# 64-token attention: the length product of a rotation one step later, its logarithm and exponential behind the next pair's exponentials

## The reference, cut to what matters

```python
h = shift_token(x)
q, k, v = split(h @ wqkv)               # 8 heads of 64
q = q / clip(norm(q, axis=-1), 1e-12) * qs   # the length of each head's row
k = k / clip(norm(k, axis=-1), 1e-12) * ksc
q, k = rotary_xpos(q, k)
sim = (q * 8) @ k'                      # own and previous window of 64 tokens
attn = softmax(where(mask, -big, sim))
x = x + (attn @ v) @ wo
...                                     # shift, layer norm, gated MLP
```

## Time and profile before

| | |
|---|---|
| median of 3 runs | 2924.2 us (2923.81 to 2928.21) |
| profiled execution, its time | 2927.47 us |
| its span in the trace | 2924.8 us |
| PE busy | 2709.7 us, 93% |
| DVE, ACT, POOL busy | 1950.3, 1877.3, 1051.4 us |
| rotations, lengths, pairs | 128 of each, in four layers |

### The profile page before, as it was taken

The page is one execution under the profiler, slowest core; times in us unless marked ns, Lnnn a source line. Parts: engine busy times, 40 slices in busy tenths (PEclk is TensorE's granted clock), DMA queues, the critical chain, the costliest instruction groups (busy, mean ns, idle before and its releaser), DMA issues.

```text
span 2924.8 us, 63475 instructions
## 1 busy us (share of the span) xinstructions
PE 2709.7 (93%) x24100; PEld 1851.9 (63%) x24100; DVE 1950.3 (67%) x5625; ACT 1877.3 (64%) x4404; POOL 1051.4 (36%) x876
## 2 busy tenths in 40 slices
PE   8989999978999999789999999898899998998998
PEld 5655656547888887368888887355455463554554
DVE  5554646366887885678888887675576325774774
ACT  5676767504766764157777776776687514875784
POOL 2322323202333330055555552454355013552551
PEclk8999999987999998899999999999999999999999
DMA  1010000000000000200000000310111002110210
GB/s 54 1 42 1 13 1 9 4 9 1 2 2 2 2 2 3 75 1 2 2 2 2 2 2 15 118 48 19 48 49 28 23 1 59 48 34 23 53 42 15
DMA packets 35280, 63.13 MB, mean 22 GB/s; under 512 B 11526, under 2 KB 15654, under 8 KB 33830
## 3 DMA queue, kind: packets, MB, share of 16 engines
q1 hardware_dynamic: 34982, 59.07, 7.3%
HBM read 23.48 MB, written 1.15 MB: 8 GB/s over the span
## 4 chain that ended last, share of the span: by engine, by line
PE 71%; DVE 13%; ACT 8%; issue 4%; SPq 2%; POOL 2%; DMA 1%; DVEq 0%; POOLq 0%; ACTq 0%
PE bank L787 61%; PE bank L1018 5%; PE bank L1138 3%; SPq L753 2%; PE bank L863 1%; ACT low L1344 1%; DVE low L1686 1%; ACT work L1380 1%; DVE low L1664 1%; DVE work L1629 1%; ACT work L1288 1%; DMA work<-work 1%; DVE halves L1679 1%; ACT squared L1260 1%; DVE centered L1500 1%
## 5 line engine op out<-in xcount | busy, mean ns | idle before, releaser
L1256 ACT ACTIVATE low<-bank 128x512 f32<-128x512 f32 (+3 forms) x512 | 427.9, 946 | 1.7 <-PE bank L1018 1.7
L787 PE MATMUL bank<-table_keys,halves 128*128 128x512 f32 (+3 forms) x1536 | 422.6, 384 | 0.6 <-ACT low L1344 0.5
L787 PE MATMUL bank<-work 128*64 128x128 f32 (+6 forms) x4480 | 365.3, 291 | 39.8 <-DVE work L1773 20.1
L1344 ACT ACTIVATE low<-bank,low 128x512 f32<-128x512 f32 (+23 forms) x384 | 227.2, 592 | 270.5 <-DVE low L1686 266.7
L787 PEld LDWEIGHTS bank<-work 128*64 128x64 f32 (+3 forms) x4480 | 266.1, 145 | 211.9 <-issue 152.2
L1686 DVE TENSOR_REDUCE low<-bank 128x1 f32<-128x512 f32 (+22 forms) x512 | 286.4, 570 | 104.0 <-PE bank L787 99.0
L1877 POOL TENSOR_TENSOR halves<-squared,const 128x512 fp32r<-128x512 f32 x128 | 136.9, 1069 | 518.9 <-PE bank L787 518.9
L1256 ACT ACTIVATE work<-bank 128x512 f32<-128x512 f32 (+4 forms) x389 | 199.7, 538 | 156.4 <-PE bank L787 80.0
L787 PEld LDWEIGHTS bank<-table_keys,halves 128*128 128x128 f32 x1536 | 248.6, 194 | 47.5 <-issue 14.0
L1380 ACT ACTIVATE work<-work 128x192 f32<-128x192 f32 (+1 forms) x512 | 218.7, 431 | 38.6 <-DVE work L1766 38.6
L1923 POOL TENSOR_TENSOR work<-work 128x768 f32<-128x768 f32 x128 | 187.7, 1466 | 135.7 <-DVE work L1777 135.7
(11 more groups left out here) (200 smaller groups left out, 5805.5 us busy)
## 6 DMA issues: line engine op xcount, KB each, us to landing
work<-work SPq DMA_DIRECT2D x512, 64.0 KB, 2.0
slot<-in_wW SPq DMA_DIRECT2D x4, 1605.5 KB, 6.6
slot<-in_wA SPq DMA_DIRECT2D x4, 837.0 KB, 6.1
table_low<-embv_padded SPq DMA_DIRECT2D x2, 1536.0 KB, 6.3
table<-in_dft SPq DMA_DIRECT2D x1, 3072.0 KB, 13.3
slot<-in_wE SPq DMA_DIRECT2D x2, 584.0 KB, 3.8
const<-in_const SPq DMA_DIRECT2D x1, 1094.5 KB, 5.5
squared<-in_x SPq DMA_DIRECT2D x4, 256.0 KB, 6.5
```

Source lines behind the costliest of these rows:

```text
L787: return pe.matmul(o, l, r, start=start, stop=stop)
L1256: return act.activation(dst, src, ACT.Identity)
L1344: act.activation(PR[t.G % 4][:, 0:n], bank[t.G % 2][:, 0:n], ACT.Exp, bias=NBR[:, t.G % 4:t.G % 4 + 1], accum_out=RSR[:, t.G % 8:t.G % 8 + ...
```

## The change

In the loop, w_length (the matmul of the length, on PE) of rotation r-1 is issued in the step of rotation r, between the scores of the pair and rotation r, and no longer that of rotation r behind the values. ACT's part becomes a kind of step of its own, w_inverse, and stands behind w_exps of the same step, ahead of w_heads. The prologue issues both together as it did. The bank of the length is still released by w_inverse.

```diff
             def length(r):
                 c, x, pt = items[r]
-                add("w_length", c=c, x=x, pt=pt, which=slot[r], i=r - newest_in.get(slot[r], r - C))
+                back = r - newest_in.get(slot[r], r - C)
                 newest_in[slot[r]] = r
+                return add("w_length", c=c, x=x, pt=pt, which=slot[r]), back
+
+            def inverse(r, measured):
+                c, x, pt = items[r]
+                add("w_inverse", c=c, x=x, pt=pt, which=slot[r], tile=measured[0], i=measured[1])
...
                 if 1 <= j <= lane_items:
-                    length(j - 1)
+                    inverse(j - 1, length(j - 1))
...
                 if j < len(pairs):
                     lane, i, hp = pairs[j]
                     add("w_scores", c=lane, i=i, hp=hp)
+                deferred = lane_items <= r - 1 < C * lane_items
+                if deferred:
+                    measured = length(r - 1)
                 if r < C * lane_items:
                     rotate(r)
                 if j < len(pairs):
                     add("w_exps", c=lane, i=i, hp=hp)
+                if deferred:
+                    inverse(r - 1, measured)
...
                         add("w_values_on", c=lane, i=i, hp=hp, u=first + j - 2, tile=held)
                         add("w_heads", c=lane, hp=hp, tile=held)
-                if r < C * lane_items:
-                    length(r)
                 if lane_items <= r - 2 < C * lane_items:
                     scale(r - 2)
...
-            def w_length(s):
-                act.wait_ge(tile_full, s.k + 1)
-
-                act.activation(tile_of(s.k)[:, :], tile_of(s.k)[:, :], ACT.Ln, bias=eps_col[:, 1:2], scale=2.0 ** 30)\
+            def w_inverse(s):
+                act.wait_ge(tile_full, s.tile.k + 1)
+                o = tile_of(s.tile.k)[:, :]
+                act.activation(o, o, ACT.Ln, bias=eps_col[:, 1:2], scale=2.0 ** 30)\
                     .then_inc(sem("w_log"), 1)
                 act.wait_ge(sem("w_log"), s.n + 1)
                 reached(act, "w_scaled", s.n - s.i + 1)
-                act.activation(RNW[:, s.which, :], tile_of(s.k)[:, :], ACT.Exp, bias=eps_col[:, 2:3], scale=-0.5)\
+                act.activation(RNW[:, s.which, :], o, ACT.Exp, bias=eps_col[:, 2:3], scale=-0.5)\
                     .then_inc(sem("w_inverse"), 1)
```

## The result

The changed kernel takes 2997.4 us (median of 4 runs, 2978.4 to 2998.6) where the kernel before takes 2924.0 (2921.5 to 2928.2): 1.0233 times as long, 95% interval 1.0196 to 1.0271. Run again later beside other kernels it took 2995.5 us against 2919.5: 1.0257 (1.0237 to 1.0276). The forecast was 2993.5 us, in a range of 2962 to 3018.

What follows compares the result with a forecast made beforehand. PE was taken to bound the kernel. Bank waits of 70.8 us less 3.5 us of idle PE, plus 2 us at the starts, gave 69.3 us on 2924.2: 2993.5 us, range 2962 to 3018.

Steps and rivals of the forecast that it cites:

- What binds: PE bounds the kernel; in steps 2 to 23 of the four attention layers it idles only 3.5 us of 472.9.
- The ring: In the loop the length's bank is held until ACT's exponential ends, so PE stalls: 70.8 us for four layers.
- no extra, even / odd: Loop steps without an extra tile: the next length waits 1.04 us (even, 3 steps a layer) or 1.25 (odd, 4).
- value alone, even / odd: Loop steps with one value product: the next scores wait 1.03 us (even, 2 steps a layer) or 1.14 (odd, 6).
- value and norm: Even loop steps with value and norm product: the next scores wait 0.17 us, 4 steps a layer, 0.68 us.
- the list: Added PE waits by kind of step, steps 2 to 22: 17.7 us a layer, 70.8 for four.
- The start: At each layer's loop start the square after step 1 comes 0.5 us later: 2 us for four layers.
- The end: Behind step 23 the length waits, but PE idles 1.45 us for ACT anyway: 0, 1 us a layer either way.
- The clock: Full clock taken in the loop; rival: it swings, one step in three at the lower level, 126 us more, 3120; 7%.
- Half of the waits: Rival: in the loop only the length's waits bind, 7 steps a layer, 32.5 us more, 2957; 6%.
- no wait: Rival: no wait on the bank in the loop, old gaps gone, each start gains 1.15 us: 2916; 4%.
- no effect: Rival: the idle time moves from one place to another that is as little used: 2924; 4%.

Runs made afterwards that it cites:

- ACT's order: Changed kernel with logarithm and exponential of the length ahead of the pair's four exponentials, banks untouched: 2938.5 us, 1.0050 of the kernel before.
- The old step 0: Changed kernel with the length of rotation 8 and its activations back in their old place in the loop's first step: 2980.3 us, 1.0211 of the kernel before.

## Why the prediction was right

**What binds.** That PE had 3.5 us of idle time in the loops, so nothing to win, holds: the order with the inverse ahead of the square takes 117.5 us for the 21 steps from 2 to 23 that took 118.2.

**The ring.** Named as the length's bank, closed by the exponential, seen by the scores after a step with an extra tile and by the length after one without. The trace has both. One bank for the length takes away 27.5 us of the loops' 62.8, as expected (28); two banks and ACT's order take away every wait for the exponential in the loop, but 18 and 9 us come back, mostly as waits for ACT's copies, which I had not foreseen; with the inverse ahead of the square too, all is gone. Predicted and measured step lengths, from square to square:

| step | predicted | measured |
|---|---|---|
| no extra, even / odd | 5.68 / 5.79 | 5.64 / 5.74 |
| value alone, even / odd | 6.53 / 6.54 | 6.51 / 6.52 |
| value and norm | 6.53 | 6.47 |
| w_out | no wait | 8.03 (8.07 to 8.26 before) |

The predicted ones are the waits of the list on top of PE's own time. The loops were to gain 67.3 us and gained 62.8. Two terms were off in opposite ways: PE resumes 0.14 us behind the exponential, not 0.06, but from the length product to the square it is then 1.99 us (1881.47 to 1883.46, into step 3), not 2.12, as the rotation runs right behind another product of its kind; and the steps with w_out became 0.04 to 0.23 us shorter.

**The start.** The term that failed: 2 us, measured 8.7. The square of step 1 came 4.22 us behind that of step 0, as worked out (4.24). But then PE reaches the turn of pair 0 and waits 2.0 us for POOL's weighing, where before it waited 1.85 us for the square, ahead of the length product that then stood between rotation and turn. I had looked at the waits of the length and the rotation and not at the turn, and had taken the full clock. It is the clock that made the size: in the four windows together PE idles 1.2 us more and is busy 7.5 us more (37.4 against 29.9) with the same matmuls. The granted clock is 0.73 in all four, where it was 1.00, 0.85, 0.85 and 1.00. In the first layer the turn, the scores and the length product, which took 0.82, 0.82 and 1.13 us, are at half the clock:

```profile
1871.55 1.54 PE L1146 MATMUL bank<-const,work 128*128 128x128 f32 x6 [2.04 <-POOL work L1931]
1873.02 1.44 PE L795 MATMUL bank<-work 64*128 64x128 f32 x8
1874.39 2.07 PE L795 MATMUL bank<-centered,const 128*128 128x512 f32 x2
```

The old step 0 takes nearly all of this back (42.4 us), so in the changed kernel the moved length goes with the loss. But neither the order nor the gap settles the clock. The kernel with the inverse ahead of the square, whose length is moved as well, was profiled twice. In both executions PE waits 2.04 us for the weighing in the first layer; the turn behind it takes 1.54 us in the first and 0.87 us in the second:

```profile
1863.40 0.87 PE L1146 MATMUL bank<-const,work 128*128 128x128 f32 x6 [2.04 <-POOL work L1931]
```

And the kernel before with its exponential twice, with the old step 0, has starts of 49.7 us. What decides the clock there stays open.

**The end.** I put it at 0; behind the last square 3.9 us were added in the profiled execution, at a lower clock with the same work. The second profile of the changed kernel has the same end (90.7 us at 0.91), and so nearly has the one with its exponential twice (93.2 at 0.91); all other versions took 86.5 to 89.8 us at 0.97 to 1.00. So this may belong to the change, by way of the clock, and the forecast had no term for it; no experiment here settles it. The 3.4 us of the other sign are not part of the mechanism: 2.2 of them lie ahead of the first layer's loop, and they were 4.8 us in the second profile.

**The total**, 2997.4 for 2993.5, is closer than its parts: 4.5 us too many in the loops, 6.7 too few at the start, and the clock outside. The mechanism was right, and its size in the loops to 7%; that the sum came within 4 us is in part luck.

**The clock.** In the loop it stayed at 1.00 with 15 gaps of about 1 us in a layer, as I took it from the earlier trace rows. The Trainium skill's warning ("TensorE: Matmul & The Clock Gate", section "A second HAM failure mode: psum-queue depth-cycling") did not come true in the loop of the changed kernel (mean clock 1.00); with the gaps 0.7 us longer it did in part (0.94 to 0.96). The price that I gave this rival was worked out for 88 steps; squares of steps 2 to 23 bound 84 in the four layers, so PE's work in a step is 5.59 us and not 5.34, which changes no chance.

**The side rivals.** Half of the waits, no wait, and no effect are ruled out by the 16.0 us of idle PE in a layer, all released by the exponential.

## What to carry to other kernels

A buffer that is written early and read late is a ring: add up, from the write, all that stands ahead of its last reader in that reader's queue, and compare it with what the writer does until it wants the buffer again. Moving the write up without moving the read up lengthens that by every instruction between; moving both up cost nothing here. Look for the next ring before you trust a cure: here the value's bank was 0.4 us behind the length's, and the kernel before had 0.01 us to spare in its odd steps with a value.

## What the runs showed that I had not expected

- Idle ACT did not help ACT's ring: with 1.4 to 2.0 us idle ahead of the squares, 0.70 us more work cost 0.71 to 0.72 us in each of the waiting steps.
- The granted clock stayed at full level through four loops with 15 gaps of 0.94 to 1.21 us each. Behind gaps of 1.77 and 2.04 us it fell in some places, where two matmuls of 128x512 take 1.9 to 2.1 us instead of 1.0 to 1.1, and not in others: in two executions of one kernel, the same wait of 2.04 us was followed by a turn of 1.54 and of 0.87 us.
- The price of a start depends on it: of the 9.7 to 12.9 us before and after the change, PE is busy for 6.7 us at a mean clock of 1.00, 8.2 to 8.3 at 0.85 and 9.2 to 9.6 at 0.73, for the same matmuls.
